# Second self-attention: additive mask and maximum in one VectorE instruction, scores kept in SBUF, and VectorE's head groups written out

## The chip, the cores and the metric

One Trainium2 chip, of which the kernel uses one core. The metric is the device time of one execution in microseconds (us). The kernel before was run three times; the median is 2108.53 us. A further execution was profiled, and all rows below come from it.

## The reference, cut to what matters

The program is a decoder of two layers on 2 sequences of 512 tokens with 512 channels. The change touches only the self-attention of the second layer. It has 16 heads of width 128 and a causal mask:

```
q = einsum(x, W_Q) + b_Q ; k = einsum(x, W_K) + b_K ; v = einsum(x, W_V) + b_V      # per head
scores = q @ k.T / sqrt(128)
scores = where(causal, scores, -1e5)
out    = softmax(scores) @ v           # then times W_O per head, summed over the heads, + b_O
x      = layernorm(x + out)
```

## The kernel before, in words

The function is `phase_attn1`. The 16 heads are taken in four groups of four heads; with the two sequences a group has eight units (`uu` = 0 to 7), called heads here. Group 0 is written out; groups 1 to 3 are a hardware loop on SyncE, GpSimd and ScalarE, and on TensorE and VectorE groups 1 and 2 are a loop and group 3 is written out.

Every value that TensorE multiplies is split into two float16 parts, a high and a low one, so each product is three matmuls (`products`, lines 77 to 79). The engines' order is written out by hand, with semaphores:

- `qk(u, j)`: TensorE makes q (j = 0) or k (j = 1) of the next head, 12 matmuls of 512 columns each. ScalarE copies it out twice with the bias (`q32`, then `Qh`, lines 1848 and 1850), and VectorE makes the low part `Ql` (line 1927). The next head's scores wait for that.
- `scores(u, qt)`: for query tile qt (128 queries) TensorE makes scores against (qt + 1) x 128 keys in one of two PSUM banks, and a fourth matmul of 128 columns adds the triangle of the mask to the last 128 keys (line 1736, the "mask product": the triangle in bfloat16 as weights, the identity streamed). Tile qt may not start before the exponential of tile qt - 2 has read the same bank (`exp_done`).
- `maximum`: VectorE takes the negated maximum along the keys from PSUM (line 1967) and scales it by SC in a second instruction of one column (line 1970). ScalarE then takes exp(SC x score + bias) out of PSUM into the SBUF buffer `Pr`, with the row sum as second output (line 1877).
- `inverse`, `normalize`: VectorE inverts the row sum and scales `Pr` (lines 1952, 1958). `turn`: TensorE transposes `Pr` (line 1744); ScalarE and VectorE split the result into `PTh` and `PTl` (lines 1884, 1975). `values`: TensorE multiplies with V; ScalarE copies out (lines 1860, 1862) and GpSimd makes the low part `Zl` (line 1699). `output`: after the eighth head of a group TensorE multiplies the group with W_O.

TensorE's order in a head is: scores 0, scores 1, qk(next, 0), scores 2, scores 3, turn of tiles 0 and 1, qk(next, 1), values of the previous head, turn of tiles 2 and 3. In the eighth head the projections are replaced by values and by output tiles.

VectorE also splits the weights of the coming group, in instructions of 2048 columns (lines 1561 and 1571): high parts after heads 1 and 3, low parts (line 1571) after heads 2 and 4.

At the start of the phase TensorE waits for two casts of mask triangles on VectorE (`const_done`, lines 2023 and 2024), ScalarE waits for a third VectorE instruction that scales the biases (line 2026), and GpSimd adds b_O to x in eight instructions (line 1706, `shifted`). SyncE issues all DMAs, the biases first.

The first self-attention of the program (lines 2045 and on) already takes its mask and maximum as the change does here (line 2449, instruction CUSTOM_DVE_ANT_0, which the profile follows with a DVE_READ_ACCUMULATOR2_ANT); its exponential (line 2356) reads SBUF.

Of the kernel before, what the change touches and what calls it, by code (L numbers as in the profile page):

```python
# [21 lines left out]
ALU = mybir.AluOpType  # L22
ACT = mybir.ActivationFunctionType
# [1608 lines left out]
def phase_attn1(c, front, cross, **end):  # L1632
# [10 lines left out]
    EARLY = NT - 2  # L1643
    SC = 1.0 / float(np.sqrt(DQK)) / (XS * XS)
    with ExitStack() as ctx:
        sb = lambda name, shape, dt: c.sb(ctx, name, shape, dt)
# [7 lines left out]
        bq = sb("bq", [P, 3, H], F32)  # L1654
        tri = cross.tri
        Qh = sb("Qh", [P, 2, 2, S], F16)
# [5 lines left out]
        Zl = sb("Zl", [P, GH, B * S], F16)  # L1662
        nmax = sb("nmax", [P, 2 * QT], F32)
        nbias = sb("nbias", [P, 2 * QT], F32)
        rsum = sb("rsum", [P, 2 * QT], F32)
        rinv = sb("rinv", [P, 2 * QT], F32)
        bias_in, const_done, shifted = sem("bias_in"), sem("const_done"), sem("shifted")
        qk_done, qk_act, qk_lo = sem("qk_done"), sem("qk_act"), sem("qk_lo")
        s_done, max_done, bias_done = sem("s_done"), sem("max_done"), sem("bias_done")
        exp_done, inv_done, norm_done = sem("exp_done"), sem("inv_done"), sem("norm_done")  # L1670
# [6 lines left out]
        @block.sync  # L1677
        def _(sp):
            def load(g):
                for i in range(4):  # L1680
                    need(sp, w_lo, 4 * (g - 1) + i + 1)
                    front.load(sp, g, i)
            sp.dma_start(bq[:], c.inp["attn1_bT"]).then_inc(bias_in, 16)
            front.load(sp, 0, 3)
            cross.load_values(sp, 0)
            cross.load_keys(sp, 0)
            with sp.Fori(1, NG) as g:
                load(g)
            sp.wait_ge(norm.xt_lo, QT)
            cross.load_queries(sp, 0)  # L1690
            norm.store(sp)
# [20 lines left out]
        def _(pe):  # L1712
# [13 lines left out]
            def scores(u, uu, qt):  # L1726
                q = uu % 2
                if qt == 0:
                    pe.wait_ge(qk_lo, 2 * u + 2)
                need(pe, exp_done, QT * u + qt - 1)  # L1730
                w = (qt + 1) * P
                out = c.PS[:, 2 + qt % 2, 0:w]
                tok = slice(qt * P, (qt + 1) * P)
                products(pe, out, (Qh[:, q, 0, tok], Ql[:, q, 0, tok]),
                         (Qh[:, q, 1, 0:w], Ql[:, q, 1, 0:w]), stop=False)
                pe.matmul(c.PS[:, 2 + qt % 2, w - P:w], c.identb[:], tri[:], start=False, stop=True,
                          skip_group_check=True).then_inc(s_done, 1)

# [21 lines left out]
            def output(g, t):  # L1760
# [14 lines left out]
                if isinstance(g, int) and g == NG - 1 and t >= 3:  # L1775
                    if t == 3:
                        pe.wait_ge(exp_done, QT * U * NG)
                    norm.pe_step(pe, t - 1)
# [10 lines left out]
            def body(g):  # L1789
# [37 lines left out]
                for t in range(3, NT):  # L1827
                    output(g, t)
            pe.wait_ge(const_done, 2)
            body(0)  # L1830
# [7 lines left out]
        def _(act):  # L1838
# [31 lines left out]
            def exp(u, uu, qt):  # L1870
                i = (uu % 2) * QT + qt
                w = (qt + 1) * P
                act.wait_ge(bias_done, QT * u + qt + 1)
                need(act, t_done, QT * (u - 1) + qt + 1)
                if isinstance(u, int) and u == 0 and qt >= 2:
                    act.wait_ge(shifted, NT)
                nc.scalar.activation(Pr[:, qt, 0:w], c.PS[:, 2 + qt % 2, 0:w], ACT.Exp, bias=nbias[:, i:i + 1],  # L1877
                                     scale=SC, accum_out=rsum[:, i:i + 1]).then_inc(exp_done, 1)

# [8 lines left out]
            def body(g):  # L1888
# [25 lines left out]
                z_out(g, U * g + U - 1, U - 1)  # L1914
            act.wait_ge(const_done, 3)
            body(0)
# [6 lines left out]
        def _(dve):  # L1923
# [40 lines left out]
            def maximum(u, uu, qt):  # L1964
                i = (uu % 2) * QT + qt
                dve.wait_ge(s_done, QT * u + qt + 1)
                nc.vector.tensor_reduce(nmax[:, i:i + 1], c.PS[:, 2 + qt % 2, 0:(qt + 1) * P], AX.X, ALU.max,
                                        negate=True).then_inc(max_done, 1)
                dve.wait_ge(max_done, QT * u + qt + 1)
                nc.vector.tensor_scalar(nbias[:, i:i + 1], nmax[:, i:i + 1], SC, None, ALU.mult).then_inc(bias_done, 1)  # L1970

# [7 lines left out]
            def body(g, more):  # L1979
# [36 lines left out]
                for t in range(1, NT):  # L2016
                    add_output(g, t)
                    if not more:
                        if t == 1:
                            norm.dve_step(dve, 0)  # L2020
                        norm.dve_step(dve, t)
            dve.wait_ge(front.const_in, 48)
            nc.vector.tensor_copy(cross.triT[:], front.triT32[:]).then_inc(const_done, 1)
            nc.vector.tensor_copy(tri[:], front.tri32[:]).then_inc(const_done, 1)  # L2024
            dve.wait_ge(bias_in, 16)
            nc.vector.tensor_scalar(bq[:], bq[:], XS, None, ALU.mult).then_inc(const_done, 1)
            body(0, True)
            with dve.Fori(1, NG - 1) as g:
                body(g, True)
            body(NG - 1, False)  # L2030
            norm.late(norm.dve_step, dve)

# [1085 lines left out]
def constants():  # L3118
# [12 lines left out]
        "c_tri": causal,  # L3131
        "c_triT": causal.T,
        "c_shift": np.full((2, Cross1Front.GS * S2), -Cross1Front.MS, np.float16).view(np.float32),

# [62 lines left out]
```

## Time and profile before

| | us |
|---|---|
| median of 3 runs (lowest to highest) | 2108.53 (2105.29 to 2111.03) |
| profiled execution, whole | 2107.33 |
| its span | 2105.6 |
| TensorE (PE) busy | 1917.6 (91%) |
| VectorE (DVE) busy | 1338.3 (64%) |
| ScalarE (ACT) busy | 1085.0 (52%) |
| GpSimd (POOL) busy | 638.0 (30%) |
| the second self-attention | from 944 to about 1440 of the span |

The span is the time between the first and the last instruction of the profile; the execution's time holds 1.73 us more. Busy times of TensorE overlap, since its matmuls are pipelined: the time that a matmul occupies is the distance from its start to the next one's start. Idle times stand in the rows in square brackets, with what ended them.

### The profile page before, as it was taken

The numbers are of one execution on the slowest core, as the hardware profiler recorded it, in microseconds if no ns is written. First come the engines' busy times: TensorE is split into PE (matmuls) and PEld (weight loads), VectorE is DVE, ScalarE is ACT, GpSimd is POOL, SyncE is SP. The second block draws the span as 40 slices with busy tenths as digits, with TensorE's granted clock in tenths as the row PEclk, the third lists the DMA queues.
The fourth block names the chain that finished last, engine by engine and source line by source line (L and its number), as shares of the span: only waits on it lengthen the run. The fifth ranks groups of instructions, "written<-read, shape, count | busy, mean of one in ns | idle before, by whom it ended". The sixth has DMA issues, their size and how long they took to land. (4 is left out here: it accounts for less than half of the span.)

```text
span 2105.6 us, 35999 instructions
## 1 busy us (share of the span) xinstructions
PE 1917.6 (91%) x12824; PEld 1185.5 (56%) x12824; DVE 1338.3 (64%) x2579; ACT 1085.0 (52%) x2135; POOL 638.0 (30%) x558
## 2 busy tenths in 40 slices
PE   7999769989999999989999999998888876999998
PEld 4666534468887788844545454453555552455553
DVE  6777665465565755676658476687899846454333
ACT  4777543243333433356536264473799973344333
POOL 4666311123333333212101011010576740133220
PEclk9999979989999999999999999998799968999999
DMA  5000023111110111205011100003500004566433
GB/s 187 27 27 2 1 109 118 46 52 50 50 50 26 50 50 41 67 22 145 21 40 41 41 20 1 1 1 76 133 3 2 2 27 149 181 181 180 122 70 96
DMA packets 103178, 131.96 MB, mean 63 GB/s; under 512 B 8264, under 2 KB 61640, under 8 KB 103008
## 3 DMA queue, kind: packets, MB, share of 16 engines
q1 hardware_dynamic: 96304, 114.20, 17.6%
q0 software_dynamic: 6720, 15.73, 3.8%
q8 instruction: 94, 1.54, 0.3%
q14 instruction: 60, 0.49, 0.1%
HBM read 103.83 MB, written 22.87 MB: 60 GB/s over the span
## 5 line engine op out<-in xcount | busy, mean ns | idle before, releaser
L1113 POOL TENSOR_TENSOR wl<-stage,wh 128x512 fp32r<-128x512 f32 x80 | 116.0, 1475 | 271.9 <-DVE wh L1108 271.9
L2890 POOL TENSOR_TENSOR PTl<-P,PTh 128x512 f16<-128x512 f32 (+2 forms) x160 | 148.8, 937 | 121.1 <-ACT PTh L3014 118.4
L1699 POOL TENSOR_TENSOR Zl<-z,Zh 128x512 f16<-128x512 f32 x32 | 51.1, 1597 | 428.0 <-ACT Zh L1862 428.0
L3013 ACT ACTIVATE P<-PS 128x512 f32<-128x512 f32 (+3 forms) x256 | 143.7, 561 | 43.2 <-PE PS L2958 42.6
L77 PE MATMUL PS<-XTh,wh 128*128 128x512 f16 x416 | 159.2, 383 | 7.4 <-DVE tri L2024 5.4
L78 PE MATMUL PS<-XTl,wh 128*128 128x512 f16 x416 | 158.9, 382 | 0.0
L79 PE MATMUL PS<-XTh,wl 128*128 128x512 f16 x416 | 158.7, 381 | 0.0
L3014 ACT ACTIVATE PTh<-PS 128x512 f16<-128x512 f32 (+3 forms) x256 | 145.4, 568 | 0.0
L3030 DVE TENSOR_REDUCE M<-PS 128x1 f32<-128x640 f32 (+3 forms) x128 | 127.0, 1012 | 4.4 <-PE PS L2942 4.4
L1351 ACT ACTIVATE h<-PS,bup 128x512 f32<-128x512 f32 x64 | 44.1, 689 | 147.0 <-PE PS L79 146.3
L2958 PE MATMUL PS<-QS,KS 98*128 98x512 f16 (+3 forms) x256 | 99.6, 390 | 18.6 <-ACT PTh L3014 14.2
L1427 DVE TENSOR_TENSOR Hl<-h,Hh 128x512 fp32r<-128x512 f32 x64 | 48.3, 759 | 100.5 <-ACT Hh L1353 99.9
L77 PE MATMUL PS<-wh,Gh 128*128 128x512 f32 x256 | 103.6, 405 | 5.0 <-ACT s L1375 5.0
L1877 ACT ACTIVATE Pr<-PS,nbias 128x128 f32<-128x128 f32 (+3 forms) x128 | 67.6, 528 | 74.7 <-DVE nbias L1970 72.9
L77 PE MATMUL PS<-XRh,wh 128*128 128x512 f32 x256 | 101.3, 396 | 3.7 <-PEq L130 2.3
L79 PE MATMUL PS<-wh,Gl 128*128 128x512 f32 x256 | 102.0, 399 | 0.0
L78 PE MATMUL PS<-wl,Gh 128*128 128x512 f32 x256 | 101.9, 398 | 0.0
L79 PE MATMUL PS<-XRh,wl 128*128 128x512 f32 x256 | 100.9, 394 | 0.0
L78 PE MATMUL PS<-XRl,wh 128*128 128x512 f32 x256 | 100.9, 394 | 0.0
L2976 PE MATMUL PS<-Vh,PTh 128*128 128x33 f16 x832 | 92.8, 184 | 6.6 <-DVE mt L3037 6.6
L2890 DVE TENSOR_TENSOR PTl<-P,PTh 128x512 f16<-128x512 f32 (+1 forms) x96 | 74.5, 776 | 35.1 <-ACT PTh L3014 32.7
L77 PE MATMUL PS<-WB,th 128*128 x240 | 91.0, 379 | 3.8 <-issue 2.9
(381 smaller groups left out, 5893.5 us busy)
## 6 DMA issues: line engine op xcount, KB each, us to landing
stage<-in_ffn_W SPq DMA_DIRECT2D x18, 1024.0 KB, 5.2
stage<-in_ffn_Wg SPq DMA_DIRECT2D x9, 1024.0 KB, 5.2
stage<-in_ffn_Wup SPq DMA_DIRECT2D x16, 512.0 KB, 3.9
stage<-in_ffn_Wdn SPq DMA_DIRECT2D x16, 512.0 KB, 3.7
wq<-in_attn_wq SPq DMA_DIRECT2D x4, 1024.0 KB, 6.6
C<-in_ctx SPq DMA_DIRECT2D x8, 512.0 KB, 8.3
stage<-in_ffn_Wsw SPq DMA_DIRECT2D x16, 256.0 KB, 3.4
stage<-in_attn_WV SPq DMA_DIRECT2D x16, 256.0 KB, 4.5
```

The source lines that it names most:

```text
L77: pe.matmul(out, a[0], b[0], start=start, stop=False, skip_group_check=True)
L78: pe.matmul(out, a[0], b[1], start=False, stop=False, skip_group_check=True)
L79: return pe.matmul(out, a[1], b[0], start=False, stop=stop, skip_group_check=True)
L1113: self.c.nc.gpsimd.tensor_tensor(self.piece(self.low[q], ch), self.piece(self.stage, ch), plain(self.piece(self.high[q], ch)), ALU.subtrac ...
L1699: nc.gpsimd.tensor_tensor(Zl[:, hh, to], z32[:, uu % 2, :], Zh[:, hh, to], ALU.subtract).then_inc(z_lo, 1)
L1877: nc.scalar.activation(Pr[:, qt, 0:w], c.PS[:, 2 + qt % 2, 0:w], ACT.Exp, bias=nbias[:, i:i + 1], scale=SC, accum_out=rsum[:, i:i + 1]).th ...
L2890: ops.tensor_tensor(PTl[:, (CT * n + kt) % RING, cols], P32[:, (CT * n + kt) % SLOTS, cols], PTh[:, (CT * n + kt) % RING, cols], ALU.subtr ...
L2958: last = pe.matmul(bank[:, q0:S], KS[g][0:R + 2, h, kt * P:(kt + 1) * P], QS[g][0:R + 2, h, q0:S], start=True, stop=(kt < K0), skip_group_ ...
L2976: pe.matmul(z_bank(n)[:, qt, :], PTh[:, slot, q], hi, start=(kt == 0 and qt == 0), stop=False, skip_group_check=True)
L3013: nc.scalar.activation(P32[:, i % SLOTS, cols], c.PS[:, 4 + i % 2, cols], ACT.Exp, scale=SC)
L3014: nc.scalar.activation(PTh[:, i % RING, cols], c.PS[:, 4 + i % 2, cols], ACT.Exp, scale=SC).then_inc(exp_done, 1)
L3030: nc.vector.tensor_reduce(M[:, n // GS, n % GS, qt:qt + 1], c.PS[:, 2 * (i % 2):2 * (i % 2) + 2, :].rearrange("p a b -> p (a b)")[:, 0:w], ...
```

## The change

Mask and maximum become one instruction on VectorE. It reads the raw scores from PSUM and a float32 mask `causal` (128 x 512, zeros and then the triangle) from SBUF, writes the masked and negated scaled scores, one value per element, into `Pr`, and gives the smallest value of each row as second output, which is the bias. The exponential then reads `Pr` and writes it in place. The fourth matmul of each score tile goes. TensorE waits for the maximum where it waited for the exponential. VectorE waits, before it writes `Pr`, for the transposes of the previous head, and in the very first head for GpSimd's eight additions; ScalarE had these two waits. At the start TensorE waits for no mask any more, ScalarE only for the scaled biases; SyncE issues one more DMA (256 KB, the mask). The four groups of VectorE are all written out.

```diff
+    FAR = 3.0e38
-        tri = cross.tri
+        causal = sb("causal", [P, S], F32)
             sp.dma_start(bq[:], c.inp["attn1_bT"]).then_inc(bias_in, 16)
+            sp.dma_start(causal[:], c.inp["c_causal"]).then_inc(causal_in, 16)
@@ tensor: scores
-                need(pe, exp_done, QT * u + qt - 1)
+                need(pe, max_done, QT * u + qt - 1)
                 products(pe, out, (Qh[:, q, 0, tok], Ql[:, q, 0, tok]),
-                         (Qh[:, q, 1, 0:w], Ql[:, q, 1, 0:w]), stop=False)
-                pe.matmul(c.PS[:, 2 + qt % 2, w - P:w], c.identb[:], tri[:], start=False, stop=True,
-                          skip_group_check=True).then_inc(s_done, 1)
+                         (Qh[:, q, 1, 0:w], Ql[:, q, 1, 0:w])).then_inc(s_done, 1)
@@ tensor: start of the phase
-            pe.wait_ge(const_done, 2)
@@ scalar: exp
-                act.wait_ge(bias_done, QT * u + qt + 1)
-                need(act, t_done, QT * (u - 1) + qt + 1)
-                if isinstance(u, int) and u == 0 and qt >= 2:
-                    act.wait_ge(shifted, NT)
-                nc.scalar.activation(Pr[:, qt, 0:w], c.PS[:, 2 + qt % 2, 0:w], ACT.Exp, bias=nbias[:, i:i + 1],
-                                     scale=SC, accum_out=rsum[:, i:i + 1]).then_inc(exp_done, 1)
+                act.wait_ge(max_done, QT * u + qt + 1)
+                nc.scalar.activation(Pr[:, qt, 0:w], Pr[:, qt, 0:w], ACT.Exp, bias=nbias[:, i:i + 1],
+                                     scale=-1.0, accum_out=rsum[:, i:i + 1]).then_inc(exp_done, 1)
@@ scalar: start of the phase
-            act.wait_ge(const_done, 3)
+            act.wait_ge(bias_ready, 1)
@@ vector: maximum
-                nc.vector.tensor_reduce(nmax[:, i:i + 1], c.PS[:, 2 + qt % 2, 0:(qt + 1) * P], AX.X, ALU.max,
-                                        negate=True).then_inc(max_done, 1)
-                dve.wait_ge(max_done, QT * u + qt + 1)
-                nc.vector.tensor_scalar(nbias[:, i:i + 1], nmax[:, i:i + 1], SC, None, ALU.mult).then_inc(bias_done, 1)
+                need(dve, t_done, QT * (u - 1) + qt + 1)
+                if isinstance(u, int) and u == 0 and qt == 2:
+                    dve.wait_ge(shifted, NT)
+                w = (qt + 1) * P
+                nc.vector.tensor_tensor_reduce(out=Pr[:, qt, 0:w], in0=c.PS[:, 2 + qt % 2, 0:w], in1=causal[:, S - w:S],
+                                               scale=-SC, scalar=FAR, op0=ALU.add, op1=ALU.min,
+                                               accum_out=nbias[:, i:i + 1]).then_inc(max_done, 1)
@@ vector: start of the phase and groups
+            dve.wait_ge(bias_in, 16)
+            nc.vector.tensor_scalar(bq[:], bq[:], XS, None, ALU.mult).then_inc(bias_ready, 1)
             dve.wait_ge(front.const_in, 48)
             nc.vector.tensor_copy(cross.triT[:], front.triT32[:]).then_inc(const_done, 1)
-            nc.vector.tensor_copy(tri[:], front.tri32[:]).then_inc(const_done, 1)
-            dve.wait_ge(bias_in, 16)
-            nc.vector.tensor_scalar(bq[:], bq[:], XS, None, ALU.mult).then_inc(const_done, 1)
-            body(0, True)
-            with dve.Fori(1, NG - 1) as g:
-                body(g, True)
-            body(NG - 1, False)
+            nc.vector.tensor_copy(cross.tri[:], front.tri32[:]).then_inc(const_done, 1)
+            dve.wait_ge(const_done, 2)
+            dve.wait_ge(causal_in, 16)
+            for g in range(NG):
+                body(g, g < NG - 1)
```

## Rows read from the trace of the kernel before

**Rows 1.** Busy times by stretch: PE, PEld, DVE, ACT, POOL, then clock and DMA.
```profile
1048.00:1177.00 129.00, 122.48 (x690) 63.81 (x690) 85.02 (x201) 64.39 (x152) 13.29 (x9) 1.00 0.11 34
```
**Rows 2.** Waits from 940 to 1445: total us, times, longest us.
```profile
ACT Pr L1877 <- DVE nbias L1970: 72.9, 53, 2.2
...
PEld PS L77 <- ACT Pr L1877: 15.8, 28, 1.5
...
PE PS L77 <- DVE tri L2024: 5.4, 1, 5.4
```
**Rows 3.** Timeline, TensorE: start us, duration us; mask product and its successor.
```profile
1098.22 0.22 PE L1736 MATMUL PS<-tri,identb 128*128 128x128 bf16 x1
...
1098.27 0.38 PE L77 MATMUL PS<-Qh 128*128 128x512 f16 x1
```
**Rows 4.** Timeline of head 1 of group 1, from qk to the next head.
```profile
1097.51 0.38 PE L79 MATMUL PS<-XTh,wl 128*128 128x512 f16 x1
...
1099.43 0.69 DVE L1927 TENSOR_TENSOR Ql<-q,Qh 128x512 f16<-128x512 f32 x1 [1.88 <-ACT Qh L1850]
...
1100.04 0.55 DVE L1967 TENSOR_REDUCE nmax<-PS 128x1 f32<-128x384 f32 x1
...
1100.81 0.58 ACT L1877 ACTIVATE Pr<-PS,nbias 128x384 f32<-128x384 f32 x1 [1.41 <-DVE nbias L1970]
...
1101.60 0.69 ACT L1877 ACTIVATE Pr<-PS,nbias 128x512 f32<-128x512 f32 x1
...
1103.84 0.69 DVE L1927 TENSOR_TENSOR Ql<-q,Qh 128x512 f16<-128x512 f32 x1 [0.41 <-ACT Qh L1850]
...
1104.66 0.23 PE L77 MATMUL PS<-Qh 128*128 128x128 f16 x1 [0.20 <-DVE Ql L1927]
```
**Rows 5.** Timeline of the first self-attention: its combined instruction and its exponential.
```profile
121.69 0.55 DVE L2449 CUSTOM_DVE_ANT_0 Pr<-PS,mask 128x384 f32<-128x384 f32 x1
...
122.28 0.61 ACT L2356 ACTIVATE Pr<-Pr,nbias 128x384 f32<-128x384 f32 x1 [0.21 <-DVE nbias L2449]
...
123.91 0.28 DVE L2449 CUSTOM_DVE_ANT_0 Pr<-PS,mask 128x128 f32<-128x128 f32 x1
...
124.23 0.40 ACT L2356 ACTIVATE Pr<-Pr,nbias 128x128 f32<-128x128 f32 x1 [1.33 <-DVE nbias L2449]
```
**Rows 6.** Timeline of head 3 of group 1, which follows a low weight part.
```profile
1118.19 0.28 DVE L1967 TENSOR_REDUCE nmax<-PS 128x1 f32<-128x128 f32 x1
...
1118.69 0.37 ACT L1877 ACTIVATE Pr<-PS,nbias 128x128 f32<-128x128 f32 x1 [2.19 <-DVE nbias L1970]
...
1119.21 0.34 PE L77 MATMUL PS<-Qh 128*128 128x384 f16 x1 [0.95 <-ACT Pr L1877]
```
**Rows 7.** Timeline of head 7 of group 1: TensorE's first output product.
```profile
1163.91 0.39 PE L77 MATMUL PS<-wh,Zh 128*128 128x512 f16 x1 [1.39 <-POOL Zl L1699]
```
**Rows 8.** Timeline of the start of the phase, and one stretch of it.
```profile
944.04 9.82 POOL L1706 TENSOR_TENSOR X<-X,bo 128x512 f32<-128x512 f32 x8 [41.39 <-POOLq L130]
...
946.53 1.27 DVE L2026 TENSOR_SCALAR bq<-bq 128x48 f32<-128x48 f32 x1
946.66 0.61 PE L77 MATMUL PS<-XTh,wh 128*128 128x512 f16 x1 [5.44 <-DVE tri L2024]
...
953.04 1.37 DVE L1927 TENSOR_TENSOR Ql<-q,Qh 128x512 f16<-128x512 f32 x1 [5.24 <-ACT Qh L1850]
...
956.31 0.23 PE L77 MATMUL PS<-Qh 128*128 128x128 f16 x1 [2.08 <-DVE Ql L1927]
...
945.00:950.00 5.00, 3.34 (x8) 1.20 (x9) 2.80 (x3) 0.00 (x0) 5.00 (x5) 0.50 0.92 284
```
**Rows 9.** Timeline, TensorE: first score matmul of head 1 (group 1), heads 1 and 2 (group 3).
```profile
1094.53 0.23 PE L77 MATMUL PS<-Qh 128*128 128x128 f16 x1 [0.46 <-DVE Ql L1927]
...
1352.22 0.23 PE L77 MATMUL PS<-Qh 128*128 128x128 f16 x1 [0.39 <-DVE Ql L1927]
...
1362.29 0.23 PE L77 MATMUL PS<-Qh 128*128 128x128 f16 x1
```

More of the change, by code:

```diff
@@ L1662, in phase_attn1 @@
         Zl = sb("Zl", [P, GH, B * S], F16)
-        nmax = sb("nmax", [P, 2 * QT], F32)
         nbias = sb("nbias", [P, 2 * QT], F32)
@@ L1666, in phase_attn1 @@
         rinv = sb("rinv", [P, 2 * QT], F32)
-        bias_in, const_done, shifted = sem("bias_in"), sem("const_done"), sem("shifted")
+        bias_in, causal_in, shifted = sem("bias_in"), sem("causal_in"), sem("shifted")
+        bias_ready, const_done = sem("bias_ready"), sem("const_done")
         qk_done, qk_act, qk_lo = sem("qk_done"), sem("qk_act"), sem("qk_lo")
-        s_done, max_done, bias_done = sem("s_done"), sem("max_done"), sem("bias_done")
+        s_done, max_done = sem("s_done"), sem("max_done")
         exp_done, inv_done, norm_done = sem("exp_done"), sem("inv_done"), sem("norm_done")
@@ L1776, in output @@
                     if t == 3:
-                        pe.wait_ge(exp_done, QT * U * NG)
+                        pe.wait_ge(max_done, QT * U * NG)
                     norm.pe_step(pe, t - 1)
@@ L3132, in constants @@
         "c_triT": causal.T,
+        "c_causal": np.concatenate([np.zeros((P, S - P)), causal], 1),
         "c_shift": np.full((2, Cross1Front.GS * S2), -Cross1Front.MS, np.float16).view(np.float32),
```

## The prediction

> **What bounds the kernel now.** I read the busy times by stretch first, to see which engine is the limit in this phase. TensorE is busy 122.5 of 129 us of a group, VectorE 85, ScalarE 64, GpSimd 13 [rows 1]: TensorE sets the pace, and only what shortens its work or its waits can count. The waits come second [rows 2]. The largest in this list, ScalarE's 72.9 us for the bias, is idle time of an engine that is not the limit and says nothing by itself. What TensorE's side waits for is smaller: 15.8 us for the exponential before a score tile, and 5.4 us once for the mask casts at the start. The third view, the timeline of one head, shows what these waits hang on, and it decides how much of each cut arrives.
>
> In the ordinary head 1 [rows 4] the reader is to see a ring. The last product of qk starts at 1097.51. ScalarE copies it out, VectorE makes Ql at 1099.43, and only then, in its own order, comes the maximum of tile 2 at 1100.04. The exponentials of tiles 2 and 3 start at 1100.81 and 1101.60, ScalarE's copies of the second projection stand behind them, Ql of that starts at 1103.84, and the next head's scores at 1104.66, after a wait of 0.20 us in the row. So TensorE is nearly full, but the end of the head is set by a chain over VectorE and ScalarE that is a little longer than TensorE's own work. From 1097.51 to 1104.66 are 7.15 us; outside this part a head is scores 0 and 1 and the first projection, which are TensorE's alone.
>
> **The change part by part.**
>
> *Mask products.* Each of the 128 occupies TensorE from 1098.22 to 1098.27, 0.053 us at the rows' resolution [rows 3]; all of them are 6.8 us. That is no sum to book. In an ordinary head the products of tiles 0 and 1 lie before the ring's start: 0.107 us on the path. Those of tiles 2 and 3 lie beside the chain: TensorE comes 0.107 earlier and waits 0.107 longer.
>
> *Maximum and bias.* Before, from the start of the 384-column maximum to its exponential pass 1100.81 - 1100.04 = 0.77 us, and for 128 columns 1118.69 - 1118.19 = 0.50 [rows 4, 6]. The combined instruction of the first self-attention takes 122.28 - 121.69 = 0.59 and 124.23 - 123.91 = 0.32 from start to exponential, readout included [rows 5]. Both lose 0.18 us. The 512-column form isn't in the trace; the maximum and the combined instruction take the same 0.55 at 384 columns, so I carry the 0.18 over. Bounds: 0 and 0.25.
>
> *Exponential from SBUF.* 0.61 us at 384 columns from SBUF [rows 5], 0.58 from PSUM [rows 4]: 0.03 more for each of two on the chain. The chain so gets 0.18 - 0.06 = 0.12 us shorter. ScalarE has slack for the rest [rows 1]. The Trainium skill ("VectorE: DVE Perf Modes", section on the TRN2 errata) speaks against this edit: it gives ScalarE a fixed cost of 224 cycles from SBUF and 172 from PSUM, which at its 1.2 GHz is 0.043 us for each. By it the chain would gain 0.09 in place of 0.12, and the total would be 0.8 us less. The rows have this very instruction in both forms, so they decide.
>
> *An ordinary head* gains 0.107 + 0.12 = 0.23 us. TensorE's wait at its end stays about as long, which is to be expected when both sides get shorter by a like amount.
>
> *Heads after a low weight part.* VectorE is late here: the maximum of tile 0 starts at 1118.19, its exponential at 1118.69, and TensorE's tile 2 at 1119.21, after 0.95 us of waiting for the exponential [rows 6]. There are 7 of these (heads 3 and 5 of groups 0 to 2, head 3 of group 3). With the wait on the maximum, TensorE starts about 0.32 + 0.1 after VectorE's start instead of 1.02, so 0.6 us sooner. But ScalarE's copy of q is behind the first two exponentials and the ring behind that: there VectorE's first maximum gives 0.18, the second another 0.12 or so after the slower exponentials have taken theirs, and the later one of tile 2 some 0.1 net. I take 0.36 us for the head; the other 0.3 of TensorE's lead becomes a longer wait for Ql at its end. Moving `exp_done` to `max_done` is worth nothing in other heads, where the exponential was done in time.
>
> *The eighth head of a group* gains nothing: TensorE waits there for PTl, then for GpSimd's Zl (1.39 us at 1163.91, [rows 7]), and the chain to it (values, two copies, the subtraction) isn't touched. Its mask products, 4 x 4 x 0.053 = 0.85 us, are given back as waiting.
>
> Sum of the heads: 32 - 4 - 7 = 21 ordinary ones x 0.23 = 4.8, and 7 x 0.36 = 2.5: 7.3 us. Bounds: 3.0 if the chain gains nothing and only 28 x 0.107 counts; 28 x (0.213 + 0.18) + 7 x 0.3 = 13 if all products and the full 0.18 counted.
>
> *The moved waits.* VectorE's wait for the previous head's transposes is met already: it has made PTl from them before. Behind it are the reciprocals and Ql, but nothing is late. The wait for GpSimd's additions comes at tile 2 of the first head; these additions run from 944.04 for 9.82 us [rows 8], so they end before that tile. If they were later, the whole ring would stand behind them; one such instruction is 1.3 us, and I count nothing.
>
> *Start of the phase.* TensorE began at 946.66 after the casts; nothing else holds it once the phase opens at about 944.04, where GpSimd's first addition starts, so it starts 2.6 us sooner. The bias instruction that ScalarE waits for becomes VectorE's first, ends by about 947.3 in place of 946.53 + 1.27 = 947.8, and is needed only near 949. The casts and the mask's DMA then run while VectorE would sit idle until Ql at 953.04. The first scores were at 956.31 [rows 8]. Two things take some back. Ql took 1.37 us at 953.04 beside GpSimd's additions, against 0.69 in rows 4, and now both of the first two Ql fall in that time: 0.7 lost. And the granted clock was 0.50 from 945 to 950, that is 1.2 GHz, after TensorE had been idle; how soon it comes back after the earlier start no row shows. If at the same moment, the twelve matmuls that now lie in the slow stretch cost half of the head start: 1.3 to 1.4 us remain; if sooner, up to 2.6. Value: 2.0. SyncE's other DMAs move back by one issue of about 0.4 us; the keys and values are for later phases.
>
> *VectorE's groups written out.* Head 1 lasts from 1094.53 to 1104.66, 10.13 us, in the loop, and 1362.29 - 1352.22 = 10.07 where TensorE and VectorE are written out [rows 4, 9]. TensorE stays in its loop, so part of 0.06 x 14 heads = 0.8: I take 0.4, with 0 and 0.9 as bounds.
>
> **Sum:** 7.3 + 2.0 + 0.4 = 9.7 us. The profiled execution took 2107.33 (its span of 2105.6 and 1.73 around it), which makes 2097.6; the median of the runs shown is 1.2 above that execution, so I say 2098. The next phases depend on nothing new and move forward as a whole. The bounds add up to 4.4 (3.0 + 1.4 + 0) and about 16.5 (13 + 2.6 + 0.9), giving 2103 to 2091 from the profiled execution, and the spread of 2105.3 to 2111.0 between equal runs comes on top.
>
> **Rivals.**
>
> *Only TensorE's own work counts.* The chain doesn't get shorter, for instance because the 512-column form is slower than the maximum it replaces and exponential 3 is held by it. For it: exponential 3 starts only 0.79 us after exponential 2, so its maximum has little room [rows 4]. Against: both known forms gain the same. 4.4 us gone: 2103 or 2104.
>
> *All of it counts.* TensorE's waits for the exponential (15.8 us, [rows 2]) vanish beside the 6.8 us of products and 2.6 at the start. Against: in rows 4 another wait stands right behind each. 2107.3 - 25.2 = 2082; half of it, which a looser ring would give, is 2090 or so.
>
> *Slower.* The combined instruction has the mask as an SBUF operand. If it gets slowed beside GpSimd as Ql is at 953.04 (0.68 us more, [rows 8]), and this falls on one of the two in the chain in each of 28 heads, it is 19 us more: 2117. It decides from 9.7 / 28 = 0.35 us per head on. Against: GpSimd is busy in only 13 of 129 us of a group, and the instruction of the first self-attention has 0.55, no more than the plain maximum [rows 4, 5]. The Trainium skill ("SBUF — State Buffer", on who interferes with whom) says that VectorE collides with GpSimd's reads where it has two SBUF inputs; this one has one, the other is in PSUM, so by that rule too the case would not arise.
>
> **How the numbers follow.** Forecast 0.66; only TensorE's own work 0.16; all or half of all 0.12; slower 0.05; that it has no effect at all 0.01. About 0.3% is what a measurement can tell, 6.3 us, so faster means below 2102.2. The forecast's case is nearly all below it, the small case mostly above: faster 0.83, same 0.12, slower 0.05. Range 2090 to 2103.5: the bounds of the terms, a little of the case in which half of all counts, and most of the small case.
>
> **What would show it.** Score tiles with three matmuls, and no 128-column bfloat16 product. In an ordinary head, 0.59 us from combined instruction to exponential and a head of 9.9 us where it was 10.13. Tile 2 after a low weight part 0.4 us behind VectorE's start, with a longer wait for Ql at the head's end. The wait for Zl in the eighth head 0.1 us longer. The first scores at about 954.3 instead of 956.31. Wrong would be a combined instruction of 512 columns above 0.8 us, an ordinary head no shorter than 10.1, or the mask's DMA or GpSimd's additions as what VectorE waits for at the start.

## Result and profile after

The median of 7 runs is 2095.57 us (2089.96 to 2103.12), against 2108.48 us for 7 runs of the kernel before. The ratio is 0.9945, with a 95% interval of 0.9924 to 0.9967. A second series of 10 runs of the same changed kernel had a median of 2095.54 and a ratio of 0.9953 (0.9933 to 0.9972). The profiled execution took 2096.02 us; its span is 2094.2, where that of before was 2105.6.

The phase is measured from GpSimd's first addition (944.04 before, 940.76 after) to the next phase's first score matmul. It went from 509.97 to 498.29 us. The phases ahead of it, which are unchanged, were 3.3 us shorter in this execution and what follows it 3.6 us longer. The profiles of the experiments show the same scatter there, so only differences within the phase are read below.

The same stretch of one group, first, from the view of busy times ([rows 1] before): the window of one group is 126.4 us wide where it was 129.0 (by the first score matmuls the group is 2.4 us shorter), and TensorE's busy time shrank by 1.8, VectorE's by 4.1.

```profile
1039.90:1166.30 126.40, 120.70 (x657) 62.34 (x656) 80.88 (x200) 63.83 (x152) 13.25 (x9) 1.00 0.12 34
```

Of the waits in the phase ([rows 2] before) the one for the exponential is gone. TensorE waits for the combined instruction instead, for under half of the time. The second row was 1.3 us before and is new as an amount: VectorE, done earlier, now idles for the row sum, which costs nothing. The last row is the new wait at the start, 3.0 us, behind which no work of TensorE stands.

```profile
ACT Pr L1873 <- DVE nbias L1967: 63.3, 50, 2.0
...
DVE rinv L1948 <- ACT Pr L1873: 12.8, 62, 0.3
...
PEld PS L77 <- DVE nbias L1967: 6.8, 7, 1.0
...
DVE bq L2022 <- DMA bq<-in_attn_bT: 3.0, 1, 3.0
```

Head 1 of group 1 again, in the order of time, with the rows that answer to [rows 4]:

```profile
1088.99 0.38 PE L79 MATMUL PS<-XTh,wl 128*128 128x512 f16 x1
...
1090.91 0.69 DVE L1923 TENSOR_TENSOR Ql<-q,Qh 128x512 f16<-128x512 f32 x1 [2.05 <-ACT Qh L1849]
1091.52 0.55 DVE L1967 CUSTOM_DVE_ANT_0 Pr<-PS,causal 128x384 f32<-128x384 f32 x1
...
1091.99 0.68 DVE L1967 CUSTOM_DVE_ANT_0 Pr<-PS,causal 128x512 f32<-128x512 f32 x1
...
1092.11 0.62 ACT L1873 ACTIVATE Pr<-Pr,nbias 128x384 f32<-128x384 f32 x1 [1.24 <-DVE nbias L1967]
...
1092.88 0.71 ACT L1873 ACTIVATE Pr<-Pr,nbias 128x512 f32<-128x512 f32 x1
...
1095.14 0.69 DVE L1923 TENSOR_TENSOR Ql<-q,Qh 128x512 f16<-128x512 f32 x1 [0.41 <-ACT Qh L1849]
...
1095.96 0.23 PE L77 MATMUL PS<-Qh 128*128 128x128 f16 x1
```

The reader is to see the ring, 1095.96 - 1088.99 = 6.97 us long where it was 7.15. From the combined instruction to the exponential are 0.59 us as forecast, where maximum and bias took 0.77. The 512-column form, unseen before, takes 0.68 us, as the maximum did.

Head 3, after a low weight part ([rows 6] before). TensorE's tile 2 now starts with the exponential instead of behind it, 0.35 us after VectorE's start instead of 1.02:

```profile
1109.14 0.28 DVE L1967 CUSTOM_DVE_ANT_0 Pr<-PS,causal 128x128 f32<-128x128 f32 x1
...
1109.47 0.40 ACT L1873 ACTIVATE Pr<-Pr,nbias 128x128 f32<-128x128 f32 x1 [2.01 <-DVE nbias L1967]
...
1109.49 0.34 PE L77 MATMUL PS<-Qh 128*128 128x384 f16 x1 [0.46 <-DVE nbias L1967]
...
1110.63 0.27 PE L1744 MATMUL PS<-ident,Pr 128*128 128x128 f32 x1
...
1111.09 0.44 PE L1744 MATMUL PS<-ident,Pr 128*128 128x128 f32 x2 [0.18 <-DVE Pr L1954]
...
1116.69 0.23 PE L77 MATMUL PS<-Qh 128*128 128x128 f16 x1 [0.17 <-DVE Ql L1923]
```

The last three rows show where TensorE's lead goes. The wait for Ql at the head's end did not get longer, as predicted, but shorter (0.17 us; before, the row below). TensorE instead waits for VectorE's `normalize` of tile 1 in the middle of its first transposes, which start 0.46 us apart here; before, the three ran without a wait:

```profile
1120.55 0.50 PE L1744 MATMUL PS<-ident,Pr 128*128 128x128 f32 x3
...
1126.28 0.23 PE L77 MATMUL PS<-Qh 128*128 128x128 f16 x1 [0.24 <-DVE Ql L1927]
```

And the eighth head's wait for Zl ([rows 7]), 0.12 us longer:

```profile
1153.43 0.39 PE L77 MATMUL PS<-wh,Zh 128*128 128x512 f16 x1 [1.51 <-POOL Zl L1701]
```

Since the heads from the second on repeat to about 0.02 us between profiles of the same kernel, their lengths are the best measure. Each is the distance between the first score matmuls of two heads, in us; the eighth runs to the next group's first.

```
                         head 0      1      2      3      4      5      6      7
before,      group 1     10.19  10.13  10.23  11.39  10.18  11.32  10.07  55.38
after,       group 1      9.81   9.85   9.81  10.92   9.79  11.05   9.77  55.45
before,      group 3     10.11  10.07  10.22  11.39   9.99  10.07   9.99
after,       group 3      9.74   9.78   9.82  10.85   9.69   9.78   9.69
```

### The profile page after: what moved, and what is told of

Read it like the earlier page. It is cut to its first block and busy times, and to the rows that moved or that the text cites. A ratio compares the mean times of both kernels' runs of the same rounds, so it can differ in the third digit from the quotient of the medians.

```text
span 2094.2 us, 35646 instructions
## 1 busy us (share of the span) xinstructions
PE 1910.9 (91%) x12696; PEld 1177.6 (56%) x12696; DVE 1325.6 (63%) x2579; ACT 1082.3 (52%) x2135; POOL 638.2 (30%) x558
## 5 line engine op out<-in xcount | busy, mean ns | idle before, releaser
L1873 ACT ACTIVATE Pr<-Pr,nbias 128x128 f32<-128x128 f32 (+3 forms) x128 | 71.0, 557 | 63.3 <-DVE nbias L1967 63.3
```

The lines of the kernel that those rows point to most:

```text
L1873: nc.scalar.activation(Pr[:, qt, 0:w], Pr[:, qt, 0:w], ACT.Exp, bias=nbias[:, i:i + 1], scale=-1.0, accum_out=rsum[:, i:i + 1]).then_inc(e ...
```

## Experiments

Whole times say less than the traces here. Against the kernel before, the ratios that are not given below were 0.9994 (0.9967 to 1.002) and 0.9998 (0.9975 to 1.0022) without mask products on tiles 0 and 1 and on tiles 2 and 3; of the changed kernel's variants, 0.995 (0.9909 to 0.999) with the wait for the exponential, 0.9934 (0.9911 to 0.9956) with the products put back, 0.9936 (0.9913 to 0.996) without GpSimd's additions, 0.9902 (0.9868 to 0.9936) with the low parts in halves and 0.9918 (0.9889 to 0.9947) with the late wait for Zl. The last two rest on three and two runs. None of the first three variants can be told from the changed kernel (0.9945 and 0.9953) by its whole time, so what follows is read from the trace.

**VectorE's groups written out, alone.** On the kernel before:

```diff
-            body(0, True)
-            with dve.Fori(1, NG - 1) as g:
-                body(g, True)
-            body(NG - 1, False)
+            for g in range(NG):
+                body(g, g < NG - 1)
```

> The kernel before, with only VectorE's groups 1 and 2 written out instead of looped. My theory, as revised by the trace after the change (the heads of group 3, which VectorE had written out already, lost 0.29 to 0.40 us each, as much as those of groups 1 and 2): writing out gives nothing in a head; heads 1 to 6 of groups 1 and 2 stay within 0.03 us of 10.13, 10.23, 11.39, 10.18, 11.32, 10.07, the whole under 0.4 us. Rival (the prediction's term): 0.03 us or more in each of 14 heads, 0.4 to 0.8 us in the sum of the heads of groups 1 and 2.

Heads 1 to 6 of group 1 sum to 63.30 us (before 63.32), those of group 2 to 63.30 (63.31). Ratio 1.0005 (0.9979 to 1.003). Writing out VectorE's groups is worth nothing. The 0.06 us that head 1 of group 3 is shorter is left to TensorE, which is in a loop in groups 1 and 2 and written out in group 3; that was not tried by itself.

**The start of the phase, alone.** On the kernel before:

```diff
                 if qt == 0:
                     pe.wait_ge(qk_lo, 2 * u + 2)
+                    if isinstance(u, int) and u == 0:
+                        pe.wait_ge(const_done, 2)
...
-            pe.wait_ge(const_done, 2)
             body(0)
...
-            act.wait_ge(const_done, 3)
+            act.wait_ge(bias_ready, 1)
...
+            dve.wait_ge(bias_in, 16)
+            nc.vector.tensor_scalar(bq[:], bq[:], XS, None, ALU.mult).then_inc(bias_ready, 1)
             dve.wait_ge(front.const_in, 48)
...
-            dve.wait_ge(bias_in, 16)
-            nc.vector.tensor_scalar(bq[:], bq[:], XS, None, ALU.mult).then_inc(const_done, 1)
```

> The kernel before, with only the start of the phase changed: TensorE waits for the mask casts only before the first score tile, ScalarE only for the scaled biases, which VectorE makes first. Theory: TensorE starts within 0.1 us of GpSimd's first addition instead of 2.6 behind it, and from GpSimd's first addition to the second head's first score matmul it is 19.8 to 20.8 us where it was 22.1; all later heads as before. Rival: the start's gain needs the rest of the change, or is given back whole in the first head: 22 us again.

TensorE starts 2.6 us sooner, and the first scores come 9.72 us after the phase's opening (GpSimd's first addition) instead of 12.27. But the second head's come after 21.27 instead of 22.14: 0.87 us is left, less than expected. Head 0 took 11.55 us instead of 9.87. The granted clock in stretches of 5 us of this kernel shows the reason (columns as in [rows 1]; the clock is the third from the end):

```profile
935.00:940.00 5.00, 4.17 (x12) 1.64 (x13) 2.29 (x3) 0.00 (x0) 4.18 (x4) 0.66 0.52 147
940.00:945.00 5.00, 2.86 (x14) 1.08 (x11) 1.73 (x2) 3.35 (x5) 5.00 (x5) 1.00 1.02 343
945.00:950.00 5.00, 4.46 (x18) 1.96 (x19) 2.39 (x9) 1.49 (x5) 1.61 (x1) 0.66 1.08 288
```

The low stretch at the opening is shorter than before (0.50 all through 945 to 950 in [rows 8]), but TensorE, done with its first 24 matmuls, then waits 2.7 us for Ql, and a second low stretch, of 3.4 us, follows within head 0. Ratio 0.9979 (0.9958 to 1.0).

**No mask products on tiles 0 and 1; none on tiles 2 and 3.** On the kernel before, for the first of the two (the second has `qt in (0, 1)`):

```diff
-                products(pe, out, (Qh[:, q, 0, tok], Ql[:, q, 0, tok]),
-                         (Qh[:, q, 1, 0:w], Ql[:, q, 1, 0:w]), stop=False)
-                pe.matmul(c.PS[:, 2 + qt % 2, w - P:w], c.identb[:], tri[:], start=False, stop=True,
-                          skip_group_check=True).then_inc(s_done, 1)
+                masked = qt in (2, 3)
+                last = products(pe, out, (Qh[:, q, 0, tok], Ql[:, q, 0, tok]),
+                                (Qh[:, q, 1, 0:w], Ql[:, q, 1, 0:w]), stop=not masked)
+                if masked:
+                    last = pe.matmul(c.PS[:, 2 + qt % 2, w - P:w], c.identb[:], tri[:], start=False, stop=True,
+                                     skip_group_check=True)
+                last.then_inc(s_done, 1)
```

> The kernel before without the mask products of tiles 0 and 1 in each head; their triangles of the mask are left out of the computation. Theory of the ring: these two products lie before the chain over VectorE and ScalarE starts, so each ordinary head (1, 2, 4, 6) gets 0.10 to 0.12 us shorter, and the eighth head does not. Rival (TensorE's sum counts wherever it is cut): the same 0.107 here, and the same again when tiles 2 and 3 are cut. Rival (the chain alone decides): 0 here.

> The kernel before without the mask products of tiles 2 and 3 in each head; their triangles of the mask are left out of the computation. Theory of the ring: they lie beside the chain, so an ordinary head gets at most 0.02 us shorter and TensorE's wait for Ql at its end 0.1 us longer. The maximum of tile 2 does not start earlier, since it stands behind Ql. Rival (TensorE's sum counts): 0.107 us per head, 3 us in all.

Lengths in group 2, us:

```
                         head 0      1      2      3      4      5      6      7
before                   10.18  10.14  10.22  11.39  10.19  11.32  10.05  55.39
no products on 0, 1      10.07  10.03  10.21  11.40  10.18  11.32   9.94  55.39
no products on 2, 3      10.18  10.14  10.11  11.26  10.19  11.26  10.06  55.27
```

The theory holds in heads 0, 1 and 6: the first pair is worth 0.11 us, the second nothing. It fails in heads 2, 3 and 5, where it is the other way round, in head 7, and in head 4, where neither pair alone gives anything. Heads 2 to 5 are those in front of which VectorE had a weight part. Group 3 bears this out: no group follows it, so its heads 4 and 5 have no weight part in front, and both behave there as the ordinary head 6 does:

```
                  group 3, head 0      1      2      3      4      5      6
before                      10.11  10.07  10.22  11.39   9.99  10.07   9.99
no products on 0, 1          9.99   9.95  10.22  11.41   9.87   9.95   9.87
no products on 2, 3         10.11  10.07  10.10  11.29   9.99  10.07   9.99
```

The second pair stands before the transposes, and these release PTl, then the weight part, then the next head's first maximum. So heads 2, 3 and 5 belong to another ring than heads 0, 1 and 6; what head 4 of groups 0 to 2 hangs on stays open. In the kernel without the second pair the second ring is to be seen in head 3 of group 2, which begins at 1249.13 - 11.26 = 1237.87:

```profile
1238.91 2.28 DVE L1571 SCALAR_TENSOR_TENSOR wl<-stage,wh 128x2048 f16<-128x2048 f32 x1
...
1242.13 0.34 PE L77 MATMUL PS<-Qh 128*128 128x384 f16 x1 [0.89 <-ACT Pr L1880]
...
1249.13 0.23 PE L77 MATMUL PS<-Qh 128*128 128x128 f16 x1 [0.23 <-DVE Ql L1930]
```

The weight part starts 1.04 us into the head. In the kernel before it is 1.11:

```profile
1243.77 0.23 PE L77 MATMUL PS<-Qh 128*128 128x128 f16 x1 [0.17 <-DVE Ql L1927]
...
1244.88 2.28 DVE L1571 SCALAR_TENSOR_TENSOR wl<-stage,wh 128x2048 f16<-128x2048 f32 x1
```

That is 0.07 of the head's 0.13. The other 0.06 comes in at ScalarE's copy of the second projection, which starts 9.14 us into the head instead of 9.27, in step with TensorE, which is 0.12 us earlier from its first transposes on.

Group 1 of this kernel is no measure: its head 1 took 11.83 us, since the granted clock was 0.50 for 3.4 us from 1087.83 on, which no other profile shows there.

**TensorE waits for the exponential again.** On the changed kernel:

```diff
-                need(pe, max_done, QT * u + qt - 1)
+                need(pe, exp_done, QT * u + qt - 1)
```

> The changed kernel, but TensorE waits again for the exponential, not the maximum, before tiles 2 and 3. Theory: only heads 3 and 5, which follow a low weight part, see it: tile 2 starts 0.5 us later there, of which the wait for Ql at the head's end (0.39 us) takes up most; heads 3 and 5 and the ones behind them get longer by 0.1 to 0.25 us, all others by 0. Rival (the earlier release is worth what it moves): 0.5 us in each of 7 heads, 3.6 us.

Heads 3, 4 and 5 of group 2 take 10.98, 9.91 and 10.98 us instead of 10.92, 9.79 and 10.94, all others the same. Over heads 1 to 6 of the four groups it is 0.93 us, 0.03 to 0.13 us in each head that is longer; for heads 3 and 5 I had expected 0.1 to 0.25. TensorE's tile 2 starts 0.59 us later in head 3 of group 2, so most of that lead was indeed slack.

**The mask products put back.** On the changed kernel (TensorE also waits again for the mask casts, before the first score tile):

```diff
-                         (Qh[:, q, 1, 0:w], Ql[:, q, 1, 0:w])).then_inc(s_done, 1)
+                         (Qh[:, q, 1, 0:w], Ql[:, q, 1, 0:w]), stop=False)
+                pe.matmul(c.PS[:, 2 + qt % 2, w - P:w], c.identb[:], cross.tri[:], start=False, stop=True,
+                          skip_group_check=True).then_inc(s_done, 1)
```

> The changed kernel with the 128 mask products put back (the triangle is then added twice, which changes nothing in the result). Revised theory, from the kernels without products of tiles 0 and 1 or of 2 and 3: each head has one pair of products on its path, the first pair in heads 0, 1 and 6, the second in heads 2, 3, 5 (through the transposes, PTl and the weight part to the next head's first maximum); so 0.10 to 0.12 us in nearly every head of 0 to 6, nothing net in the eighth: about 3 us. Rival (TensorE's sum): 0.21 us per head, 6.8 us.

Group 2: 9.93, 9.97, 9.93, 11.04, 9.88, 11.09, 9.88, 55.57. Every head of it is 0.10 to 0.14 us longer, the eighth too, which I had not expected. From the phase's first score matmul to the last head's it is 3.5 us: half of the 6.8 that TensorE streams.

**The changed kernel again, and without GpSimd's additions.** The second leaves out b_O and with it the waits on `shifted`:

```diff
-            for t in range(NT):
-                nc.gpsimd.tensor_tensor(c.X[:, t, :], c.X[:, t, :], front.bo[:], ALU.add).then_inc(shifted, 1)
```

> The changed kernel once more. From GpSimd's first addition to the second head's first score matmul its first profile showed 19.7 us with one slow stretch of TensorE's clock (from 950.1); three kernels with the same start showed 20.9 to 21.0 with two (near 944 and 954). Theory: 20.9 to 21.0 is the usual case, so the start is worth 1.2 us with its first head and not 2.5. Rival: 19.7 is the kernel's own and the others differ for another reason. The heads from the second on are to be the same within 0.02 us.

> The changed kernel without GpSimd's eight additions of b_O at the start of the phase; b_O is left out. Theory: the first two Ql, 1.66 us each in the profile of the changed kernel, take 0.69, the three small VectorE instructions ahead of them (0.96 to 1.34 us each) under 0.3, and the first scores come 1.8 to 2 us sooner after TensorE's start; a part is lost again if TensorE's clock is low then. Rival: Ql's length is the load of the DMA queues at that time, and it stays at 1.4 us or more.

The second profile of the changed kernel has its second head 20.91 us after the opening, as have six experiments with this start (20.91 to 21.10); the 19.68 of the first profile was the better case. From the second head on the two agree to 0.01 us. Without the additions the two Ql take 0.69 us, and the casts 0.22:

```profile
937.26 0.19 DVE L2016 TENSOR_SCALAR bq<-bq 128x48 f32<-128x48 f32 x1 [3.05 <-DMA bq<-in_attn_bT]
937.36 0.22 DVE L2018 CAST triT<-triT 128x128 bf16<-128x128 f32 x1
...
941.56 0.69 DVE L1921 TENSOR_TENSOR Ql<-q,Qh 128x512 f16<-128x512 f32 x1 [3.84 <-ACT Qh L1847]
...
943.98 0.69 DVE L1921 TENSOR_TENSOR Ql<-q,Qh 128x512 f16<-128x512 f32 x1 [1.73 <-ACT Qh L1847]
```

With them, in the second profile:

```profile
938.98 1.34 DVE L2024 CAST triT<-triT 128x128 bf16<-128x128 f32 x1
...
942.31 0.92 DVE L1923 TENSOR_TENSOR Ql<-q,Qh 128x512 f16<-128x512 f32 x1 [0.77 <-ACT Qh L1849]
944.73 1.39 DVE L1923 TENSOR_TENSOR Ql<-q,Qh 128x512 f16<-128x512 f32 x1 [1.50 <-ACT Qh L1849]
```

So it is GpSimd's additions and not the load of the DMA queues, which was as high in both: 295, 377 and 359 GB/s without the additions and 304, 362 and 350 with them, in stretches of 2 us from 4 us behind TensorE's start on. The gain is only 0.6 us (first scores 9.03 us after TensorE's start instead of 9.63), a third of what I expected: I had taken Ql's 1.66 us from the first profile, in which both met an addition head on.

**The low weight part cut in halves; all parts in the gap; the late wait for Zl; both.** The traces left two waits of TensorE: 0.64 us at tile 2 of heads 3 and 5, and 1.7 us in the eighth head. On the changed kernel, the second half of each low part (columns 1024 to 2047) behind `normalize(u, uu, 1)` of the next head:

```diff
+                    if uu == 3:
+                        weight_lo_half(g, 3, 1)
+                    if uu == 5 and more:
+                        weight_lo_half(g + 1, 0, 1)
```

> The changed kernel; each low weight part (2.28 us of VectorE) is cut into halves, one at the old place and one 3 us later, where VectorE idles for Ql. Theory: the first maxima of heads 3 and 5 stand behind 1.2 instead of 2.3 us, TensorE's wait of 0.64 us at tile 2 goes, and heads 3 and 5 take 9.9 to 10.2 us where they took 10.86 to 10.94: some 5 us in all for 7 heads. Rival: the second half holds up Ql and with it the chain of tile 2, and what is won ahead of it is lost behind: heads 3 and 5 stay above 10.6.

Heads 3 and 5 take 10.30 and 10.35 us in group 2, 0.6 less, but not the 10.2 or less that I expected: the first halves still stand ahead of the first maxima. Heads 1 to 6 of the four groups are 4.4 us shorter in sum. So all parts went to that place:

```diff
+                    if uu == 1:
+                        weight_hi(g, 3)
+                    if uu in (2, 3):
+                        weight_lo_half(g, 3, uu - 2)
+                    if uu == 4 and more:
+                        weight_hi(g + 1, 0)
+                    if uu in (5, 6) and more:
+                        weight_lo_half(g + 1, 0, uu - 5)
...
-                    if uu in (1, 2):
-                        (weight_hi if uu == 1 else weight_lo)(g, 3)
-                    if uu in (3, 4) and more:
-                        (weight_hi if uu == 3 else weight_lo)(g + 1, 0)
```

> The changed kernel with all weight parts of VectorE placed in the 2.05 us that it idles before Ql of the next head (high parts whole in heads 1 and 4, halves of the low parts in heads 2, 3, 5, 6). Theory: with nothing ahead of the first maxima, heads 3 and 5 lose TensorE's wait at tile 2 and heads 2 and 4 what stands ahead of theirs, and 1.2 us in a gap of 2.05 hold nothing up: heads 1 to 6 all 9.65 to 9.85 us in groups 1 and 2, their sum 58.2 to 59 where it is 61.1; some 8 us in all. Rival: the gap is needed by normalize and the copies (the half that followed head 3's first tiles ended 0.1 us before Ql and head 3 stayed at 10.3), and the heads stay above 10.

Heads 1 to 6 of group 2: 9.86, 9.77, 9.85, 9.77, 9.86, 9.77, their sum 58.88 us where it was 61.08. The half fits between the last normalize and Ql, which still waits 0.15 us for ScalarE:

```profile
1092.94 0.35 DVE L1964 TENSOR_SCALAR Pr<-Pr,rinv 128x256 f32<-128x256 f32 x1
1093.21 1.22 DVE L1942 SCALAR_TENSOR_TENSOR wl<-stage,wh 128x1024 f16<-128x1024 f32 x1
1094.58 0.69 DVE L1923 TENSOR_TENSOR Ql<-q,Qh 128x512 f16<-128x512 f32 x1 [0.15 <-ACT Qh L1849]
```

The median is 2082.76 us, ratio 0.9897 (0.9859 to 0.9934).

The other wait:

```diff
-                    pe.wait_ge(z_lo, U * g + U - 1)
-                if t == QT:
-                    pe.wait_ge(z_lo, U * (g + 1))
+                    pe.wait_ge(z_lo, U * g + U - 2)
...
                 for hh in range(GH):
+                    if hh == GH - 1 and t == 0:
+                        pe.wait_ge(z_lo, U * g + U - 1)
+                    if hh == GH - 1 and t == QT:
+                        pe.wait_ge(z_lo, U * (g + 1))
```

> The changed kernel; in the first and fifth output tile of a group TensorE waits for GpSimd's last Zl only before the fourth head's product, after nine matmuls that don't need it. Theory: the wait of 1.73 us (1.40 in group 0) and that of 0.28 (0.16) in the eighth head vanish, since nothing else of the chain is late there: from the eighth head's first score to the next group's first 53.4 to 53.6 us in groups 1 and 2 where it is 55.45. In all about 7.5 us. Rival: the transposes of tiles 2 and 3 or the additions to x then become what TensorE waits for, and under 1 us per group is left.

The eighth head takes 53.66, 53.51 and 53.52 us in groups 0 to 2 where it took 55.18, 55.45 and 55.45. The output starts right behind the transposes and no wait follows:

```profile
1155.78 0.49 PE L1744 MATMUL PS<-ident,Pr 128*128 128x128 f32 x3
1156.11 0.38 PE L77 MATMUL PS<-wh,Zh 128*128 128x512 f16 x1
```

> The changed kernel with both: the weight parts in the gap, and the wait for the last Zl moved behind nine matmuls. Theory: both gains add, 7.5 and about 8 us: some 15 us under the changed kernel, 2079 to 2084. Rival: one takes what the other gave, since the eighth head's PTl becomes the wait; under 11 us.

The phase takes 483.66 us, where the second profile of the changed kernel has 499.05, the gap alone 490.55 and the late wait alone 492.65. The gains add, 8.5 and 6.4 us against 15.4; that of the late wait is 1.1 us less than the 7.5 expected, most of it in the fourth group, which gave 1.0 us where groups 1 and 2 gave 1.9 each. The median of 4 runs is 2076.14 us (2074.65 to 2084.12), ratio 0.9854 (0.9819 to 0.9889): the fastest version here. That is 19.4 us under the changed kernel's median and below the 2079 to 2084 expected. The phase accounts for 15.4 us of this. The other 4 us lie outside it and are no more than the scatter of whole times.

## Why the prediction was right

The whole came out as predicted, 2095.6 for 2098, and the phase got shorter by 11.7 us in the first profile and 10.9 in the second, for 9.7. The mechanism, TensorE's own work with a chain over VectorE and ScalarE beside it, is what the traces show. That the sum came so close is luck in part: several of its steps were off and partly cancelled.

- *The limit.* TensorE with a chain beside it: right. Of 6.8 us of mask products 3.5 count.
- *Maximum and bias,* 0.18 us: right for every form, and the third rival's slow instruction isn't there (0.55 and 0.68 us).
- *The chain,* forecast 0.12 us shorter, came out at 0.17 to 0.18. The step that failed is "0.03 more for each of two on the chain". The exponentials did get slower, 0.62 for 0.58 and 0.71 for 0.69. But exponential 3 had also been held by VectorE: its bias, an instruction of 0.15 us from 1101.41 on in the trace, was ready at 1101.56, and it started at 1101.60 [rows 4]. Now it starts as soon as ScalarE is free, 0.77 us behind exponential 2 where it was 0.79, though exponential 2 is longer. Over the four sizes the exponential from SBUF takes 0.023 to 0.036 us more. The Trainium skill ("VectorE: DVE Perf Modes", section on the TRN2 errata) has 52 cycles between the two, an estimate of 0.043 us at 1.2 GHz: the same sign, and more than these rows show.
- *Ordinary heads,* forecast 0.23 us. Heads 1 and 6 gained 0.28 to 0.30. Heads 2 and 4 gained 0.39 to 0.47 (head 4 of group 3, with no weight part in front, 0.30): they aren't ordinary. A high weight part stands ahead of their first maxima, as the low part does in heads 3 and 5. That the first two maxima are therefore on their path is argued from this order. In heads 2, 3 and 5 the mask products that count are those of tiles 2 and 3, not of 0 and 1.
- *Heads after a low part,* forecast 0.36: 0.27 to 0.54. The step that failed is "the other 0.3 of TensorE's lead becomes a longer wait for Ql at its end": in head 3 of group 1 that wait fell from 0.24 to 0.17 us. TensorE spends the lead earlier, before the transpose of tile 1, where it waits for VectorE's `normalize`.
- *The eighth head,* forecast 0: 0.07 us longer. The wait for Zl grew by 0.12, as expected. That the products alone cost 0.11 there, as the experiments show, leaves about 0.18 that something else costs. The traces show what. In group 1, ScalarE's copy of head 6's last transposes starts 9.98 us into that head, both before and with the products put back, though the head is 0.18 shorter there. So the shorter chain brings the eighth head's first score forward, but not the transposes, on which the rest of the head hangs, and the eighth head gives that 0.18 back.
- *All heads,* forecast 7.3 us (bounds 3.0 to 13): the 27 heads behind the first gave 9.96 us, the first 0.3 to 0.4 (0.29 against the kernel with the start alone, 0.37 in the other groups), less 0.2 for the eighth ones: about 10.1. From the last head's first scores to the next phase it took 0.5 us longer in the first profile of the changed kernel and 0.1 in the second. That is scatter: in the twelve profiles without the late wait for Zl this part takes 39.96 to 40.60 us, whatever the kernel.
- *Start,* forecast 2.0 us: with head 0's own 0.3 to 0.4 taken off, 2.1 in the first profile of the changed kernel and about 0.9 in the usual case (0.87 with the start alone changed). The step that failed is the clock: I asked when it comes back, and not whether it would fall again. It fell within head 0 in all ten profiles in which TensorE starts at the opening, and in none of the four with the old start. The length of TensorE's wait for Ql just before does not explain this by itself: it was 2.6 to 3.1 us in nine of the ten, but 2.08 without the additions, as in the kernel before, where the clock did not fall. What makes it fall stays open.
- *Written out,* forecast 0.4: 0. I had put a difference down to both engines that belongs to TensorE's loop.
- *The moved waits,* forecast nothing: nothing was to be seen.

The forecast's sum stood up since two terms too large (start and loop, by 1.5 us in the usual case) met one too small (heads, by 2.8).

## What to carry to other kernels

On a pacing engine that was 95% busy, only half of the work cut from it counted (3.5 of 6.8 us): the part that lay outside what a chain over other engines set. Find the chain's starting point in the timeline and see which side each cut is on, for each kind of iteration: heads that follow a bulk operation on another engine belonged to another ring here. When a wait of the pacing engine remains, look for work already released that can go ahead of it, and put bulk work where its engine idles for something else: these two, found in the traces, gained more than the change did (15.4 us of the phase for 10.9).

## What the runs showed of the hardware that was not expected

- Beside GpSimd's additions VectorE's two-input subtraction took 0.74 to 1.68 us for 0.69 (shortest in the kernel with the late wait for Zl, longest in the first profile of the changed kernel), a cast 1.34 for 0.22, and two of the eight additions themselves 1.71 for 1.26. The combined instruction, with one input in PSUM, kept its length throughout the phase (0.28 us at 128 columns to 0.69 at 512), in the 44 of 128 cases beside a GpSimd instruction too.
- With TensorE starting at the opening, after 2.84 us of idling, the granted clock was 0.50 there for 3.4 us in seven of the eight profiles of the changed kernel and its variants with the additions, and full in one, the first of the changed kernel. In all eight it was 0.50 for another 3.4 us within head 0, after a wait of 2.6 to 3.1 us for Ql. A low stretch of that length within a head made it 1.7 us longer (11.83 us for 10.14, without the second pair of products).
- Head lengths repeat to 0.02 us from one execution to the next, unless a low stretch of the clock falls into them, while whole times of the changed kernel scatter by 13 us: what decides a change of 0.1% is read from the repeating part.
